# A Fourier neural operator on one core: the pointwise product of the inverse stage on four 64x64 tiles

## The chip, the cores and the metric

The kernel runs on one core of a Trainium2 chip. The metric is the device time of one launch in microseconds (us); lower is better. Engines are named as the profile names them: PE is TensorE (PEld its weight loads), DVE VectorE, ACT ScalarE, POOL GpSimd, SP SyncE, whose queue issues every transfer of the stages spoken of here.

## What is computed

Four layers of a Fourier neural operator on 32 images of 64x64 pixels and 64 channels, then a head, attention over 141 tokens and a mixture of experts. The change touches only the layers:

```python
h = jnp.einsum('bhwi,ic->bhwc', x, fc0_w) + fc0_b
h = h.transpose(0, 3, 1, 2)
for l in range(LAYERS):
    sc = _spectral_conv(h, w1r[l] + 1j * w1i[l], w2r[l] + 1j * w2i[l])
    pw = jnp.einsum('bihw,oi->bohw', h, pw_w[l]) + pw_b[l][None, :, None, None]
    y = sc + pw
    mean = y.mean(axis=(0, 2, 3), keepdims=True)
    var = y.var(axis=(0, 2, 3), keepdims=True)
    y = (y - mean) * jax.lax.rsqrt(var + EPS)
    y = y * gamma[l][None, :, None, None] + beta[l][None, :, None, None]
    h = jax.nn.gelu(y, approximate=False)
```

`_spectral_conv` is a real 2D FFT, a product of the 32x16 lowest modes with complex 64x64 matrices per mode, and the inverse FFT.

## The kernel before

Two images make a pair: partitions 0 to 63 hold the channels of the first, 64 to 127 those of the second, and 4096 columns hold the pixels. There are 16 pairs. Between stages the activations y lie in DRAM (`z_d`), the spectra in `X_d` and `G_d`. Each layer has three stages with a barrier between them: `fwd` (gelu of z, two forward transforms), `mix` (the product over the channels per mode) and `inv` (two inverse transforms, pointwise product, bias, statistics). Layer 0 has no `fwd` and no gelu: its z is the input x with 3 channels per image, and its pointwise weights are the product of the input layer and `pw_w`.

In `inv` a step is a quarter of a pair, 16 image rows or 1024 columns; a layer has 64 steps. Each engine runs a software pipeline written out by hand in `over_steps` and `step`: in turn n it works on step n minus a lag. All orders are fixed by this code, and semaphores carry the waits (`pI1`, `eI1`, `pT3`, `eT3`, `pY`, `eY`, `eS`, `z_gelu_c` count what PE, DVE and ACT have finished).

- PE, in each turn: four transposes of `Ai` (lag 5, line 371); in every second turn the first inverse transform (lag 1, L460), 16 matmuls of K = 64, 64 output rows and 128 columns on the four quarters of the array, `v` choosing the upper or lower half of the rows and `h`, the image, the half of the columns; then (lag 6) the pointwise product, two matmuls of K = 128 (block-diagonal weights `wbd` for two images; in layer 0 `wc6` with 96 rows) and 512 columns (L472); then the second inverse transform, eight matmuls that add to the same PSUM banks P[4] to P[7] (L477).
- DVE: copies the transposes to `ATs` (L738), the first transform from P[0] or P[1] to `Ai` (L743), and computes `bn_stats` of y (lag 7, L750).
- ACT: gelu of the loaded z in place (lag 4, L594, layers 1 to 3), then y = PSUM + bias into `ybuf` (lag 6, L604), two instructions of 512 columns per step.
- SP: in turn n, at the start of a pair four loads of `Gt` from `G_d` (L291), each 64 partitions; the store of step n - 8 from `ybuf` (L296), 128 partitions of 4 KB, after `eY`; the load of z for step n (L304; L302 for x in layer 0), after `pY` says that `zbuf` is free. `ybuf` has two buffers of one step.

Step q of a pair needs z columns q * 1024 to q * 1024 + 1023. The two PSUM banks of a step hold the upper and the lower two rows of each group of four, for both images.

## Time and profile before

| | |
|---|---|
| median of three runs | 3080.52 us (3080.41 to 3087.89) |
| the profiled execution | 3082.53 us, its span 3080.4 us |
| mean granted TensorE clock | 0.926 of full speed |
| PE busy | 2629.7 us (85%) |
| DVE busy | 1577.3 us (51%) |
| ACT busy | 1567.5 us (51%) |
| HBM read and written | 396 MB and 204 MB, 195 GB/s over the span |

The profile gives busy time per engine, the same in 40 slices of the span, the transfers, the chain of instructions that ended last, and groups of instructions by line. A PE group counts records: a matmul of float32 leaves two, a transpose one. The inverse stages lie at about 209 to 476, 789 to 1050, 1402 to 1650 and 1950 to 2215 us of the span.

### The profile page before, as it was taken

The numbers are of one execution on the slowest core, as the hardware profiler recorded it, in microseconds if no ns is written. First come the engines' busy times: TensorE is split into PE (matmuls) and PEld (weight loads), VectorE is DVE, ScalarE is ACT, GpSimd is POOL, SyncE is SP. The second block draws the span as 40 slices with busy tenths as digits, with TensorE's granted clock in tenths as the row PEclk, the third lists the DMA queues.
The fourth block names the chain that finished last, engine by engine and source line by source line (L and its number), as shares of the span: only waits on it lengthen the run. The fifth ranks groups of instructions, "written<-read, shape, count | busy, mean of one in ns | idle before, by whom it ended". The sixth has DMA issues, their size and how long they took to land. (4 is left out here: it accounts for less than half of the span.)

```text
span 3080.4 us, 65084 instructions
## 1 busy us (share of the span) xinstructions
PE 2629.7 (85%) x27131; PEld 1694.6 (55%) x27131; DVE 1577.3 (51%) x2552; ACT 1567.5 (51%) x2659; POOL 191.7 (6%) x237
## 2 busy tenths in 40 slices
PE   7559998978899899669998977899799577882999
PEld 4556665648566566566665657566422156642444
DVE  3136666752466677326666752466500376746443
ACT  1213336742456677225566753355499567851333
POOL 0000000000000000000000000000000222220443
PEclk9779999988899999889999998899899888995999
DMA  7845448966899799669988967799665200001432
GB/s 241 246 127 172 168 164 311 322 192 172 252 294 291 273 328 308 140 187 288 295 283 299 322 203 179 233 291 296 221 225 178 51 1 1 1 1 40 94 88 63
DMA packets 243649, 603.67 MB, mean 196 GB/s; under 512 B 28415, under 2 KB 108991, under 8 KB 241087
## 3 DMA queue, kind: packets, MB, share of 16 engines
q1 hardware_dynamic: 243359, 599.51, 62.7%
q8 instruction: 218, 3.57, 0.5%
q14 instruction: 72, 0.59, 0.1%
HBM read 396.12 MB, written 203.93 MB: 195 GB/s over the span
## 5 line engine op out<-in xcount | busy, mean ns | idle before, releaser
L604 ACT ACTIVATE work<-P,small 128x512 f32<-128x512 f32 x512 | 323.8, 683 | 536.0 <-PE P L477 499.3
L371 PE MATMUL P<-cst,work 128*128 128x128 f32 (+1 forms) x3760 | 547.3, 285 | 48.9 <-ACT work L626 13.7
L371 PEld LDWEIGHTS P<-cst,work 128*128 128x128 f32 (+1 forms) x3760 | 410.4, 143 | 206.6 <-issue 157.6
L426 PE MATMUL P<-W,work 128*64 128x64 f32 x4096 | 283.6, 307 | 129.9 <-ACT work L575 129.5
L472 PE MATMUL P<-work,wbd 128*128 128x512 f32 x768 | 371.5, 606 | 0.0
L477 PEld LDWEIGHTS P<-cst,ATs 64*128 64x128 f32 x4096 | 248.4, 187 | 194.1 <-issue 194.1
L426 PEld LDWEIGHTS P<-W,work 128*64 128x64 f32 x4096 | 282.0, 239 | 132.4 <-issue 98.7
L738 DVE COPY ATs<-P 128x512 f32<-128x512 f32 x256 | 177.0, 692 | 327.5 <-PE P L371 327.5
L750 DVE BATCH_NORM_STATS2 W<-work 128x6 f32<-128x512 f32 x512 | 327.1, 680 | 19.8 <-ACT work L604 19.2
L477 PE MATMUL P<-cst,ATs 64*128 64x128 f32 x4096 | 297.5, 285 | 0.0
L780 DVE COPY work<-P 128x512 f32<-128x512 f32 x384 | 247.1, 684 | 73.0 <-PE P L371 72.9
L594 ACT ACTIVATE work<-work,small 128x1024 f32<-128x1024 f32 x192 | 237.3, 1237 | 34.8 <-DMA work<-z_d 34.8
L626 ACT ACTIVATE work<-work,small 128x1024 f32<-128x1024 f32 x192 | 232.8, 1244 | 1.3 <-DMA work<-z_d 1.2
L743 DVE COPY work<-P 128x512 f32<-128x512 f32 x256 | 175.0, 686 | 110.6 <-PE P L460 110.6
L460 PE MATMUL P<-cst,work 64*64 64x128 f32 x4096 | 151.9, 289 | 55.6 <-DMA work<-G_d 49.6
L472 PEld LDWEIGHTS P<-work,wbd 128*128 128x128 f32 x768 | 131.4, 191 | 107.6 <-issue 107.3
L1463 DVE TENSOR_TENSOR mhid<-MH,ms 128x768 f32<-128x768 f32 (+1 forms) x96 | 90.4, 941 | 144.9 <-ACT ms L1389 116.9
L460 PEld LDWEIGHTS P<-cst,work 64*64 64x64 f32 x4096 | 119.1, 141 | 78.8 <-issue 61.1
L786 DVE COPY work<-P 128x512 f32<-128x512 f32 x192 | 132.7, 691 | 46.3 <-PE P L371 46.3
L719 DVE COPY work<-P 128x512 f32<-128x512 f32 x64 | 44.3, 693 | 212.3 <-PE P L426 130.9
L1134 ACT ACTIVATE aE<-AP,am 96x141 f32<-96x141 f32 x384 | 137.9, 380 | 29.0 <-DVE am L1184 28.4
L1389 ACT ACTIVATE ms<-MH 128x768 f32<-128x768 f32 (+1 forms) x96 | 76.5, 797 | 147.4 <-PE MH L1340 147.4
(166 smaller groups left out, 3031.2 us busy)
## 6 DMA issues: line engine op xcount, KB each, us to landing
work<-z_d SPq DMA_DIRECT2D x384, 512.0 KB, 6.0
z_d<-work SPq DMA_DIRECT2D x256, 512.0 KB, 4.0
W<-in_wmix SPq DMA_DIRECT2D x96, 512.0 KB, 6.8
X_d<-work SPq DMA_DIRECT2D x128, 256.0 KB, 5.0
work<-X_d SPq DMA_DIRECT2D x32, 1024.0 KB, 12.4
G_d<-work SPq DMA_DIRECT2D x128, 256.0 KB, 3.3
work<-G_d SPq DMA_DIRECT2D x256, 128.0 KB, 5.4
hz<-z_d SPq DMA_DIRECT2D x64, 512.0 KB, 4.6
```

The lines of the kernel that those rows point to most:

```text
L371: return nc.tensor.matmul(out, in_, ident[0:n, 0:n], start=True, stop=True, is_transpose=True)
L426: last = nc.tensor.matmul(P[n % 8][f * 64:f * 64 + 64, i * 64:i * 64 + 64], xm[:, :, x * 4 + y], W[:, 4 * (c + f) + y, x * 64:x * 64 + 64] ...
L460: last = nc.tensor.matmul(P[v][h * 64:h * 64 + 64, i * 128:i * 128 + 128], Gt[a.par][o, x:x + 64], i1c[o, v * 128:v * 128 + 128], start=Tr ...
L472: nc.tensor.matmul(banks[s][:, :].rearrange("p (j n) -> p j n", n=128), pw[0:rows, :], z[:, s], start=True, stop=False)
L477: last = nc.tensor.matmul(banks[s][:, j * 128:j * 128 + 128], ATs[o, a.q % 2, j * 128:j * 128 + 128], i2c[o, s * 128:s * 128 + 128], start ...
L594: nc.scalar.activation(z, z, ACT.Gelu, bias=bbi, scale=bsc).then_inc(S["z_gelu_c"], 1)
L604: nc.scalar.activation(y[:, h], P[4 + 2 * (a.q % 2) + h][:, :].rearrange("p (j n) -> p j n", n=128), ACT.Identity, bias=bias0 if first els ...
L626: nc.scalar.activation(zq[a.s % FR], zq[a.s % FR], ACT.Gelu, bias=bbi, scale=bsc).then_inc(S["z_gelu"], 1)
L738: nc.vector.tensor_copy(ATs[:, a.q % 2, :], P[2 + a.q % 2][:, :]).then_inc(S["eT3"], 1)
L743: nc.vector.tensor_copy(Ai[a.par].rearrange("p (y k) -> p y k", k=2 * KX)[:, :, v * KX + 8 * b:v * KX + 8 * b + 8], P[v][:, :].rearrange(" ...
L750: nc.vector.bn_stats(so, ybuf[a.q % 2][:, h * 512:h * 512 + 512]).then_inc(S["eS"], 1)
L780: nc.vector.tensor_copy(hTq[a.s % 2][:, h * 512:h * 512 + 512], P[h][:, :]).then_inc(S["eT1"], 1)
```

## The change

The pointwise product no longer takes two images as one block of 128 rows. Each image (`h`) and each half of the image's rows (`g`) gets its own 64x64 quarter of the array: four matmuls of K = 64 and 512 columns, with `h` choosing the rows of the array and `g` its columns. So the output partitions are now (half of the rows, channel), and a PSUM bank belongs to one image. Step q covers 8 rows of the upper half and the 8 rows 32 below.

What has to fit this layout:
- the constants `i1` are reordered and the first inverse transform (L460) runs as 32 matmuls of 64 columns instead of 16 of 128; its output partitions are (half, channel), and each group of 32 belongs to one image. DVE's copy to `Ai` takes runs of 16;
- `ybuf` has two buffers of 2048 columns, each for two steps of both images; SP stores them once in two steps, with two transfers, one from partitions 0 to 63 and one from 64 to 127 (`z_y`), so that `z_d` keeps its layout;
- z is loaded and passed to gelu in the order of columns 0, 2, 1, 3 (`QCOL`), and the product of step q waits for two gelus;
- in layer 0 x lies on partitions 0 to 2 and 64 to 66, with two loads per step, and the weights come from a product of 128x128 (`fcp`).

Core of the diff:

```diff
@@ -35,7 +35,9 @@
     f2[0, :, 0], f2[1, :, 0], f2[0, :, 1], f2[1, :, 1] = c, s, -s, c
-    i1 = np.kron(np.eye(2), np.block([[c.T, s.T], [-s.T, c.T]]))
+    i1 = np.block([[c.T, s.T], [-s.T, c.T]]).reshape(2 * KY, 2, 2, SIDE // 2).transpose(0, 2, 1, 3).reshape(2 * KY, 128)
+    i1 = np.kron(np.eye(2), i1)
     i2 = np.zeros((4, KX, 2, 4, SIDE))
@@ -112,14 +115,13 @@
         Gt = [part(14336, 1024), part(15360, 1024)]
-        ybuf = [part(16384, 1024), part(17408, 1024)]
+        ybuf = [part(12288, 2048), part(16384, 2048)]
         stats = W[:, WP - 1, 0:768]
...
         Xs0 = Xs + [part(0, 1024), part(1024, 1024)]
-        fc0Tbd = small[:, 16:22]
         fc0b_c, pwb_c, gam_c, bet_c = (small[:, i:i + 1] for i in range(4))
@@ -146,7 +148,10 @@
         z_q = z_d.rearrange("(t u) p (q n) -> t u p q n", u=2, q=4)
-        x6_q = x6.rearrange("(t u) p (q n) -> t u p q n", u=2, q=4)
+        x6_q = x6.rearrange("(t u) (h c) (q n) -> t u h c q n", u=2, h=2, q=4)
+        z_y = z_d.rearrange("(t u) (h o) (g k n) -> t u g k o h n", u=2, h=2, g=2, k=2)
+        QCOL = (0, 2, 1, 3)
@@ -196,6 +201,11 @@
+        def ychunk(a, h):
+            o = h * 1024 + a.q % 2 * 512
+            return ybuf[a.q // 2][:, o:o + 512]
         def over_steps(eng, body, last=PAIRS // 2 + 1):
@@ -290,21 +300,24 @@
                     b = At(t, u, q, 8)
-                    if b.ok:
+                    if b.ok and b.q % 2 == 1:
                         sp.wait_ge(S["eY"], l * 128 + b.s * 2 + 2)
-                        sp.dma_start(z_q[b.t, b.par, :, b.q], ybuf[b.q % 2]).then_inc(yst[b.q % 2], 16)
+                        for g in range(2):
+                            sp.dma_start(z_y[b.t, b.par, g, b.q // 2], ybuf[b.q // 2][g * 64:g * 64 + 64, :].rearrange("p (h n) -> p h n", h=2)).then_inc(yst[b.q // 2], 16)
                     if not a.ok:
                         return
-                    wait(sp, "pY", l * 128 + a.s * 2 - 14)
-                    o = slice(q * 1024, q * 1024 + 1024)
+                    if a.pair >= 2:
+                        sp.wait_ge(S["pY"], l * 128 + (a.pair - 2) * 8 + q // 2 * 4 + 4)
+                    o = slice(QCOL[q] * 1024, QCOL[q] * 1024 + 1024)
                     if first:
-                        sp.dma_start(zbuf[u][0:6, o], x6_q[a.t, u, :, q]).then_inc(zl[u][q], 16)
+                        for h in range(2):
+                            sp.dma_start(zbuf[u][h * 64:h * 64 + 3, o], x6_q[a.t, u, h, :, QCOL[q]]).then_inc(zl[u][q], 16)
                     else:
-                        sp.dma_start(zbuf[u][:, o], z_q[a.t, u, :, q]).then_inc(zl[u][q], 16)
+                        sp.dma_start(zbuf[u][:, o], z_q[a.t, u, :, QCOL[q]]).then_inc(zl[u][q], 16)
                 over_steps(sp, step)
                 for u in range(2):
-                    sp.wait_ge(yst[u], (l + 1) * 32 * 16)
+                    sp.wait_ge(yst[u], (l + 1) * 16 * 32)
                 leave(sp, "sp")
@@ -432,10 +445,10 @@
-                    nc.tensor.matmul(P[7][0:6, 0:128], fc0Tbd, wbd[:, :], start=True, stop=True)
+                    nc.tensor.matmul(P[7][:, 0:128], fcp[:, :], wbd[:, :], start=True, stop=True)
                     nc.tensor.matmul(P[6][:, 0:1], wbd[:, :], fc0b_c, start=True, stop=True).then_inc(S["pStat"], 1)
                     pe.wait_ge(S["eStat"], 1)
-                rows, pw = (96, wc6) if first else (128, wbd)
+                pw = wc6 if first else wbd
@@ -452,29 +465,30 @@
                         wait(pe, "eI1", l * 64 + a.s)
-                        for i in range(4):
-                            m = 2 * a.q + i
-                            for h in range(2):
+                        for m in range(8):
+                            for g in range(2):
                                 for v in range(2):
-                                    o, x = slice(v * 64, v * 64 + 64), h * 512 + m * 64
-                                    last = nc.tensor.matmul(P[v][h * 64:h * 64 + 64, i * 128:i * 128 + 128], Gt[a.par][o, x:x + 64], i1c[o, v * 128:v * 128 + 128], start=True, stop=True)
+                                    o, x, k = slice(v * 64, v * 64 + 64), a.q // 2 * 512 + m * 64, v * 128 + g * 64
+                                    last = nc.tensor.matmul(P[v][g * 64:g * 64 + 64, m * 64:m * 64 + 64], Gt[a.par][o, x:x + 64], i1c[o, k:k + 64], start=True, stop=True)
                         last.then_inc(S["pI1"], 1)
...
                         if first:
-                            pe.wait_ge(zl[a.par][a.q], a.t * 16 + 16)
+                            pe.wait_ge(zl[a.par][a.q // 2 * 2], a.t * 32 + 32)
+                            pe.wait_ge(zl[a.par][a.q // 2 * 2 + 1], a.t * 32 + 32)
                         else:
-                            pe.wait_ge(S["z_gelu_c"], (l - 1) * 64 + a.s + 1)
+                            pe.wait_ge(S["z_gelu_c"], (l - 1) * 64 + a.pair * 4 + a.q // 2 * 2 + 2)
                         wait(pe, "eY", l * 128 + a.s * 2 - 2)
                         banks = P[4 + 2 * (a.q % 2):6 + 2 * (a.q % 2)]
-                        z = zbuf[a.par][0:rows, a.q * 1024:a.q * 1024 + 1024].rearrange("p (j s n) -> p s j n", s=2, n=128)
-                        for s in range(2):
-                            nc.tensor.matmul(banks[s][:, :].rearrange("p (j n) -> p j n", n=128), pw[0:rows, :], z[:, s], start=True, stop=False)
+                        for g in range(2):
+                            for h in range(2):
+                                o, x = slice(h * 64, h * 64 + 64), g * 2048 + a.q * 512
+                                nc.tensor.matmul(banks[h][g * 64:g * 64 + 64, :], pw[o, o], zbuf[a.par][o, x:x + 512], start=True, stop=False)
                         pe.wait_ge(S["eT3"], l * 64 + a.s + 1)
                         for j in range(4):
-                            for s in range(2):
-                                o = slice(s * 64, s * 64 + 64)
-                                last = nc.tensor.matmul(banks[s][:, j * 128:j * 128 + 128], ATs[o, a.q % 2, j * 128:j * 128 + 128], i2c[o, s * 128:s * 128 + 128], start=False, stop=j == 3)
+                            for h in range(2):
+                                o = slice(h * 64, h * 64 + 64)
+                                last = nc.tensor.matmul(banks[h][:, j * 128:j * 128 + 128], ATs[o, a.q % 2, j * 128:j * 128 + 128], i2c[o, h * 128:h * 128 + 128], start=False, stop=j == 3)
                                 if j == 3:
@@ -588,20 +602,20 @@
                     c = At(t, u, q, 4)
-                    z = zbuf[c.par][:, c.q * 1024:c.q * 1024 + 1024]
+                    z = zbuf[c.par][:, QCOL[c.q] * 1024:QCOL[c.q] * 1024 + 1024]
                     if c.ok and not first:
-                        wait(act, zl[c.par][c.q], l * 128 + c.t * 16 + 16)
+                        wait(act, zl[c.par][c.q], 256 + (l - 1) * 128 + c.t * 16 + 16)
                         nc.scalar.activation(z, z, ACT.Gelu, bias=bbi, scale=bsc).then_inc(S["z_gelu_c"], 1)
...
                     if a.ok:
-                        y = ybuf[a.q % 2].rearrange("p (j s n) -> p s j n", s=2, n=128)
                         for h in range(2):
                             act.wait_ge(S["pY"], l * 128 + a.s * 2 + h + 1)
-                            if h == 0:
-                                wait(act, yst[a.q % 2], stores_waited(l, a))
-                                wait(act, "eS", l * 128 + a.s * 2 - 2)
-                            nc.scalar.activation(y[:, h], P[4 + 2 * (a.q % 2) + h][:, :].rearrange("p (j n) -> p j n", n=128), ACT.Identity, bias=bias0 if first else pwb_c).then_inc(S["eY"], 1)
+                            if h == 0 and a.pair >= 1:
+                                if a.q % 2 == 0:
+                                    act.wait_ge(yst[a.q // 2], (l * 16 + a.pair) * 32)
+                                act.wait_ge(S["eS"], l * 128 + a.s * 2 - 6)
+                            nc.scalar.activation(ychunk(a, h), P[4 + 2 * (a.q % 2) + h][:, :], ACT.Identity, bias=bias0 if first else pwb_c).then_inc(S["eY"], 1)
                 if first:
@@ -740,14 +750,14 @@
                         dve.wait_ge(S["pI1"], l * 32 + a.pair * 2 + b + 1)
-                        nc.vector.tensor_copy(Ai[a.par].rearrange("p (y k) -> p y k", k=2 * KX)[:, :, v * KX + 8 * b:v * KX + 8 * b + 8],
-                                              P[v][:, :].rearrange("p (k y) -> p y k", y=SIDE)).then_inc(S["eI1"], 1)
+                        nc.vector.tensor_copy(Ai[a.par].rearrange("p (y h z k) -> p h y z k", h=2, z=2, k=2 * KX)[:, b, :, :, v * KX:v * KX + KX],
+                                              P[v][:, :].rearrange("p (k y z) -> p y z k", k=KX, z=2)).then_inc(S["eI1"], 1)
                     a = At(t, u, q, 7)
...
                             so = stats.rearrange("p (t c) -> p t c", c=96)[:, a.t, a.par * 48 + (a.q * 2 + h) * 6:a.par * 48 + (a.q * 2 + h) * 6 + 6]
-                            nc.vector.bn_stats(so, ybuf[a.q % 2][:, h * 512:h * 512 + 512]).then_inc(S["eS"], 1)
+                            nc.vector.bn_stats(so, ychunk(a, h)).then_inc(S["eS"], 1)
                 over_steps(dve, step)
```

PE's instructions over two turns in the middle of layer 0, before (`wc` is the weight tile `wc6`, P the PSUM banks; x16 counts matmuls):

```order
L472 MATMUL P<-work,wc 128x512 x2
L477 MATMUL P<-cst,ATs 128x128 x8
L371 MATMUL P<-cst,work 128x128 x4
L460 MATMUL P<-cst,work 64x128 x16
L472 MATMUL P<-work,wc 128x512 x2
L477 MATMUL P<-cst,ATs 128x128 x8
L371 MATMUL P<-cst,work 128x128 x4
L472 MATMUL P<-work,wc 128x512 x2
```

and with the change, the same two turns, where the line numbers are those of the changed file:

```order
L486 MATMUL P<-work,wc 64x512 x4
L491 MATMUL P<-cst,ATs 128x128 x8
L384 MATMUL P<-cst,work 128x128 x4
L472 MATMUL P<-cst,work 64x64 x32
L486 MATMUL P<-work,wc 64x512 x4
L491 MATMUL P<-cst,ATs 128x128 x8
L384 MATMUL P<-cst,work 128x128 x4
L486 MATMUL P<-work,wc 64x512 x4
```

The order stays. Each product is four matmuls of 64 output rows instead of two of 128, each first transform 32 matmuls of 64 columns instead of 16 of 128.

SP's queue over one pair of images in layer 1, before (L291 loads the spectra, L296 stores y, L304 loads z):

```order
L291 DMA work<-G_d 64x512 [waits pI1]
L291 DMA work<-G_d 64x512 x3
L296 DMA z_d<-work 128x1024 [waits eY]
L304 DMA work<-z_d 128x1024 [waits pY]
L296 DMA z_d<-work 128x1024 [waits eY]
L304 DMA work<-z_d 128x1024 [waits pY]
L296 DMA z_d<-work 128x1024 [waits eY]
L304 DMA work<-z_d 128x1024 [waits pY]
L296 DMA z_d<-work 128x1024 [waits eY]
L304 DMA work<-z_d 128x1024 [waits pY]
```

and with the change:

```order
L301 DMA work<-G_d 64x512 [waits pI1]
L301 DMA work<-G_d 64x512 x3
L317 DMA work<-z_d 128x1024 [waits pY]
L307 DMA z_d<-work 64x2x1024 [waits eY]
L307 DMA z_d<-work 64x2x1024
L317 DMA work<-z_d 128x1024 [waits pY] x2
L307 DMA z_d<-work 64x2x1024 [waits eY]
L307 DMA z_d<-work 64x2x1024
L317 DMA work<-z_d 128x1024 [waits pY]
```

The eight transfers of z of a pair stay eight, and the loads of `G_d` stay four. The stores come two at a time after every second step, each from 64 partitions with two runs of 1024 columns, between two loads.

## Rows read from the trace of the kernel before

**Rows 1.** The page, parts 1 to 3: engines, 40 slices, the transfer queue.

```profile
PE 2629.7 (85%) x27131; PEld 1694.6 (55%) x27131; DVE 1577.3 (51%) x2552; ACT 1567.5 (51%) x2659; POOL 191.7 (6%) x237
...
PEclk9779999988899999889999998899899888995999
DMA  7845448966899799669988967799665200001432
...
q1 hardware_dynamic: 243359, 599.51, 62.7%
```

**Rows 2.** The view of stretches: 32 us of each inverse stage, layers 0 to 3.

```profile
core 0: us, PE busy (x) PEld busy (x) DVE busy (x) ACT busy (x) POOL busy (x), PEclk, DMA share, GB/s
262.00:294.00 32.00, 32.00 (x322) 19.76 (x322) 20.13 (x33) 10.12 (x16) 0.00 (x0) 1.00 0.49 170
862.00:894.00 32.00, 31.93 (x321) 19.88 (x320) 20.08 (x33) 19.13 (x24) 0.00 (x0) 1.00 0.93 295
1482.00:1514.00 32.00, 32.00 (x321) 19.79 (x320) 20.13 (x33) 19.03 (x25) 0.00 (x0) 1.00 0.93 296
2118.00:2150.00 32.00, 32.00 (x321) 19.81 (x320) 20.23 (x32) 19.13 (x24) 0.00 (x0) 1.00 0.94 301
```

**Rows 3.** The view of waits: who waited for whom, us in total, times, longest.

```profile
engine line waited for: us in total, times, longest us
...
ACT work L604 <- PE P L477: 499.3, 241, 32.7
```

**Rows 4.** Timeline of PE, two steps of layer 1; start us, duration us.

```profile
start us, us, engine line op out<-in xcount [idle before <-releaser]
907.00 0.66 PE L371 MATMUL P<-cst,work 128*128 128x128 f32 x4
907.58 1.10 PE L460 MATMUL P<-cst,work 64*64 64x128 f32 x32
908.62 1.98 PE L472 MATMUL P<-work,wbd 128*128 128x512 f32 x4
910.53 1.16 PE L477 MATMUL P<-cst,ATs 64*128 64x128 f32 x16
911.62 0.66 PE L371 MATMUL P<-cst,work 128*128 128x128 f32 x4
912.12 1.88 PE L472 MATMUL P<-work,wbd 128*128 128x512 f32 x4
913.93 1.16 PE L477 MATMUL P<-cst,ATs 64*128 64x128 f32 x16
915.02 0.66 PE L371 MATMUL P<-cst,work 128*128 128x128 f32 x4
915.61 0.34 PE L460 MATMUL P<-cst,work 64*64 64x128 f32 x4
```

**Rows 5.** Timeline of PE elsewhere: groups of matmuls on several tiles of the array.

```profile
621.35 0.66 PE L512 MATMUL P<-work,cst 64*32 64x256 f32 x16
...
1799.87 1.09 PE L534 MATMUL P<-work,cst 64*32 64x256 f32 x32
...
2302.04 1.06 PE L919 MATMUL HO<-hg,hfz 128*32 128x512 f32 x8
```

**Rows 6.** Groups by shape (busy us, mean ns); the last row is the timeline of L1329.

```profile
L426 PE MATMUL P<-W,work 128*64 128x64 f32 x4096 | 283.6, 307 | 129.9 <-ACT work L575 129.5 <-issue 0.4
...
L512 PE MATMUL P<-work,cst 64*32 64x256 f32 x3072 | 128.6, 392 | 1.9 <-DVE work L780 1.9
...
L1329 PE MATMUL MO<-mfold,macc 128*96 128x64 f32 x94 | 10.5, 254 | 0.5 <-ACT macc L1381 0.5
...
2899.29 0.89 PE L1329 MATMUL MO<-mfold,macc 128*96 128x64 f32 x8
```

**Rows 7.** The page, part 6: transfers by tile, KB of one, median us to landing.

```profile
work<-z_d SPq DMA_DIRECT2D x384, 512.0 KB, 6.0
z_d<-work SPq DMA_DIRECT2D x256, 512.0 KB, 4.0
```

**Rows 8.** Timeline: a load of x in layer 0; the start of layer 1.

```profile
245.29 0.32 SPq L302 DMA_DIRECT2D work<-in_x  x1
...
476.29 2.96 SPq L312 DMA_DIRECT2D work<-z_d  x6
...
482.81 2.37 ACT L626 ACTIVATE work<-work,small 128x1024 f32<-128x1024 f32 x2
```

**Rows 9.** Stretches: loads of 128 partitions, of 0 to 63; G_d, X_d stores; forward.

```profile
1646.00:1656.00 10.00, 9.47 (x107) 6.18 (x106) 6.67 (x11) 7.03 (x9) 0.00 (x0) 0.79 1.03 415
690.00:697.00 7.00, 0.16 (x2) 0.19 (x4) 2.12 (x2) 3.48 (x2) 0.00 (x0) 0.50 1.00 204
712.10:713.40 1.30, 1.30 (x24) 1.30 (x23) 0.69 (x1) 0.87 (x1) 0.00 (x0) 1.00 0.99 202
713.40:714.30 0.90, 0.90 (x18) 0.90 (x17) 0.00 (x0) 0.00 (x0) 0.00 (x0) 1.00 0.82 291
55.00:75.00 20.00, 19.01 (x42) 7.29 (x41) 7.77 (x20) 5.92 (x10) 0.00 (x0) 1.00 0.96 244
500.00:530.00 30.00, 30.00 (x492) 20.24 (x484) 22.90 (x42) 21.26 (x34) 0.00 (x0) 1.00 0.93 327
```

More of the change, by code:

```diff
@@ L84, in build_fno @@
         wbd = sb("wbd", [128, 128])
-        wc6 = sb("wc6", [96, 128])
+        wc6 = sb("wc6", [128, 128])
+        fcp = sb("fcp", [128, 128])
         P = [ctx.enter_context(nc.psum_tensor(f"P{i}", [128, 512], f32)) for i in range(8)]
@@ L236, in _ @@
                 o = slice(h * 64, h * 64 + 64)
-                sp.dma_start(fc0Tbd[o, h * 3:h * 3 + 3], fc0T).then_inc(S["s_w0"], 16)
+                sp.dma_start(fcp[o, h * 64:h * 64 + 3], fc0T).then_inc(S["s_w0"], 16)
                 sp.dma_start(fc0b_c[o, :], fc0b).then_inc(S["s_w0"], 16)
@@ L350, in _ @@
             nc.gpsimd.memset(small[:, :], 0.0)
-            nc.gpsimd.memset(wc6[:, :], 0.0)
+            nc.gpsimd.memset(fcp[:, :], 0.0)
             nc.gpsimd.memset(wbd[:, :], 0.0).then_inc(S["s_zero"], 1)
@@ L611, in inv @@
                 leave(act, "act")
-            def stores_waited(l, a):
-                return l * 32 * 16 + (a.pair * 2 + a.q // 2) * 16 if a.s >= 2 else 0
             def fwd(l):
@@ L725, in inv @@
                     dve.wait_ge(S["pStat"], 1)
-                    nc.vector.memset(work[0:96, 0:8192], 0.0).then_inc(S["z_zero"], 1)
+                    nc.vector.memset(work[:, 0:8192], 0.0).then_inc(S["z_zero"], 1)
                     dve.wait_ge(S["s_zero"], 2)
-                    link(nc.vector.tensor_copy(wc6[0:6, :], P[7][0:6, 0:128]))
+                    link(nc.vector.tensor_copy(wc6[:, :], P[7][:, 0:128]))
                 dve.wait_ge(S["s_parload"], (l + 1) * 128)
```

## Prediction

> **What bounds the kernel now.** I read the page first: PE is busy 85% of the span, DVE and ACT 51% each, and the DMA row stands at 8 or 9 tenths over long stretches [rows 1]. A share of the whole says little, so the next view is the table of stretches over the four inverse stages, the only ones that the change alters. In a steady 32 us of each, PE is busy for all of it at a granted clock of 1.00. In layer 0 the DMA engines stand at 0.49. In layers 1 to 3, which also read z back, they stand at 0.93 and 295 to 301 GB/s [rows 2]. PE is the bound there, and DMA is the next one, 7% behind. The waits agree: ACT's biggest wait is for the last inverse transform on PE [rows 3].
>
> The timeline gives the rhythm [rows 4]. Two steps, one with the first transform and one without, last from 907.58 to 915.61, so 8.03 us; 32 such pairs make a layer. Within a pair PE spends 1.04 us from start to start in the first transform (L460), then 1.91 and 1.81 us in the two pointwise products (L472), about 1.1 in each second transform (L477) and the rest in transposes (L371). DVE and ACT need about 20.1 and 19.0 us of 32, 5.0 and 4.8 per pair [rows 2].
>
> **The change on PE.** Pointwise product: two matmuls of 128x128 weights and 512 columns become four of 64x64 and 512 columns on the four quarters of the array. Each matmul leaves two records. The old form takes 1.88 to 1.98 us for its four records, because they follow one another [rows 4]. The nearest form with four tiles is L919 of the head, four column tiles of 512 columns: its eight records take 1.06 us. L460 shows that quarters of 64x64 overlap too (32 records in 1.10 us), and L534 that tiles may read different columns of the same partitions (32 records of 256 columns in 1.09 us) [rows 4, 5]. With the 0.07 us by which the next group starts before a row ends, a product costs 0.99 us and the pair saves 0.92 + 0.82 = 1.74 us. If the quarters did not overlap, eight records one after another would cost about 3.8 us per product; these three rows exclude it.
>
> First transform: 16 matmuls of 128 columns become 32 of 64 columns, 64 records for 32. The columns are the same in sum. Lower bound: nothing added. Upper bound: L426, also 64 columns wide, with 69 ns per record (283.6 us for 4096) on two tiles; with four that is 35 ns, 64 records take 2.2 us, and 1.2 us is added. Between them lies L1329: one tile, 64 columns but 96 columns of weights, (0.89 - 0.25) / 7 = 0.09 us each [rows 6]. Scaled to 64 columns of weights and spread over four tiles this is 0.015 us, or 0.97 us for 64 records, no more than the 1.04 of now. I take zero. The Trainium skill (TensorE: Matmul & The Clock Gate, Back-to-back issue gap) puts a floor of about 25 ns under small matmuls; 64 of them would be 1.6 us, and the sum for layer 0 would be 18 us less favourable. L512 does not bear it out: its 16 records last 0.66 us together and 0.39 us each, so they start within 0.27 us, 18 ns apart [rows 5, 6].
>
> Modes: the gap between L460 and L472 goes, and one between transposes and product comes in each step, where now the product starts 0.16 us before the transposes' row ends, against 0.08 for L460 [rows 4]. I put +0.08 us per pair. PE needs 8.03 - 1.74 + 0.08 = 6.37 us per pair.
>
> **What hides the rest.** The DVE copy of the first transform writes runs of 16 instead of 8 from a PSUM read that stays strided; the ACT eviction has the same 512 elements per partition. Both cost nothing, under PE's 6.37 us against 5.0 and 4.8. The product of step s now needs the gelu of s + 1, which ACT runs one turn earlier. The set-up (one wider memset, one 128-column product) happens once. The queue on SP keeps its twelve issues per pair of images in layers 1 to 3, but the store waits for two steps, and the load ahead of it for one step more of PE. Loads are issued six turns before their gelu; a store has one turn more than before until its buffer is needed, about 3 x 3.2 - 1.3 = 8 us even at PE's new pace, against a landing of 4.0 us for one of 512 KB [rows 7]. In layer 0 the small loads double, from one issue to two, each 0.32 us of SP. At the end of a layer the last store is twice as large and the next stage's loads wait for it. They are issued at 476.29 and ACT's first gelu starts at 482.81, behind the statistics, so with a landing of 6.0 us the cover is about 0.5 us [rows 7, 8]; without it a layer loses 1 to 2 us. I leave this out of the sum.
>
> **The change on the DMA engines.** Bytes stay the same: 295 GB/s x 8.03 us = 2.37 MB per pair of steps. Their present need is 0.93 x 8.03 = 7.47 us in layers 1 to 3 and 0.49 x 8.03 = 3.93 us in layer 0. But each store now covers 64 partitions instead of 128, 1.05 MB per pair. Loads over all partitions run at 415 GB/s with the engines full; loads into partitions 0 to 63 run at 204 GB/s, also full. G_d's stores, which come in halves, run at 202 GB/s for partitions 0 to 63 and at 291 for 64 to 127, and X_d's, which alternate the halves in 512-byte packets, at 244 [rows 9]. So the price x of the halves, per pair: below, nothing (the 291 GB/s is no half, and X_d beats 204); above, 1.05 / 0.204 - 1.05 / 0.415 = 2.6 us. G_d's two stores of 0.26 MB took 1.30 + 0.90 us; four of these are 4.4 us against 2.5, so x = 1.9 for stores that stand alone. In a queue that is never empty, one half's packets run beside the other's and beside full-width loads; I take a third of it, x = 0.6. This is the least certain number here. The need becomes 7.47 + 0.6 = 8.07 us in layers 1 to 3, above PE's 6.37: **DMA becomes the bound, at the old pace**. In layer 0 it is 4.5, still under PE.
>
> The Trainium skill speaks against the change here (SBUF — State Buffer, Door 1): partitions 0 to 63 reach only 8 of the 16 ports, and two transfers on the two halves do not add up. By that rule every half store runs at half rate, which is the 2.6 us above. The load row of 204 GB/s agrees with it; the store row of 291 does not.
>
> **The sum.** Layer 0: 32 x (6.37 - 8.03) = -53 us. Layers 1 to 3: 96 x (8.07 - 8.03) = +4. Together -49. The profiled execution took 3082.5 us (span 3080.4), 2.0 above the median of 3080.5: 3033.5 against itself, 3031 against the median.
>
> **The rivals.**
> Half stores cost their isolated price (slower). With x = 1.9 the DMA need is 9.37 us, layers 1 to 3 lose 96 x 1.34 = 129 us, layer 0 still gains 53, and the time is 3157. With x = 2.6 it is 10.07 us, +196, and layer 0 gains 48: 3229. It decides where 96 (x - 0.56) passes 53, at x = 1.11. For it: G_d's first halves and the loads into one half [rows 9]. Against it: G_d's second half, and X_d. Chance 0.33.
> The halves cost nothing and the queue packs better. The forward stage holds 327 GB/s over 30 us [rows 9]; at that rate a pair takes 2.37 / 0.327 = 7.25 us, layers 1 to 3 gain 75, the sum is -128: 2952. Were DMA no bound at all, 128 x 1.66 = 212 would come off: 2868. Chance 0.20.
> The first transform pays its upper bound: PE 7.57 us, layer 0 gains 15 and the others stay: about 3069. Chance 0.05. If the tiles did not overlap, each pair would grow by some 4 us and the kernel by 500; under 0.01.
> Gain and loss cancel (x near 1.1), between 3071 and 3090: 0.08.
> The forecast, 3005 to 3070: 0.34.
>
> **The numbers.** A measurement of this kernel can tell 0.3%, 9 us, from no change. Faster: 0.34 + 0.20 + 0.05 = 0.59. Same: 0.08. Slower: 0.33. The range must reach into both big rivals: 2940 takes in the better queue, 3165 the isolated price; outside are the unbound case and the full half rate, 2 in 10. The forecast's own range is 3005 to 3070.
>
> **What would show it.** Right: a pair of 6.3 to 6.5 us in layer 0 with PE still busy throughout; product rows of eight records near 1.0 us; in layers 1 to 3 a pair near 8.1 us, DMA share at 1.0, PE with gaps, and ACT's eviction waiting for the z_d store. Wrong: layers 1 to 3 well under 7.6 us per pair (the halves are free), or over 8.4 with the DMA rate under 280 GB/s (they are not); a first transform over 1.5 us; or a layer 0 that waits for anything but PE.

## The result, and the profile after

The kernel with the change takes **3182.4 us** (median of 4 runs, 3177.7 to 3184.6) against 3082.0 for the kernel before on the same chip: ratio 1.032, 95% interval 1.030 to 1.034. It is slower by 100 us, where 3031 was forecast, and outside the forecast's outer range of 2940 to 3165.

The profiled execution has a span of 3175.6 us. The page, parts 1 and 6, beside [rows 1] and [rows 7]:

```profile
PE 2511.6 (79%) x32251; PEld 1645.9 (52%) x32251; DVE 1576.0 (50%) x2552; ACT 1567.9 (49%) x2659; POOL 191.7 (6%) x237
...
z_d<-work SPq DMA_DIRECT2D x256, 512.0 KB, 6.1
```

PE does its work in 118 us less than before, so the arithmetic was saved, and the time still grew. The store of 512 KB lands in 6.1 us instead of 4.0 [rows 7].

The view of stretches, from the first to the last y eviction of each inverse stage, layers 0 to 3. Counted in evictions such a stretch has 31.6 pairs of steps, and that is the divisor of the figures per pair below, unless a middle is named. The loads and first transforms of the first steps stand ahead of the stretch, so these figures come out some per cent under the steady rhythm (250.04 / 31.6 = 7.91 for the 8.03 of [rows 4]):

```profile
core 0: us, PE busy (x) PEld busy (x) DVE busy (x) ACT busy (x) POOL busy (x), PEclk, DMA share, GB/s
221.15:445.79 224.64, 202.01 (x3616) 129.64 (x3615) 155.84 (x246) 80.24 (x128) 0.00 (x0) 0.98 0.74 182
781.46:1066.65 285.19, 223.08 (x3616) 143.33 (x3616) 155.88 (x246) 148.92 (x188) 0.00 (x0) 0.87 0.84 241
1401.62:1687.69 286.07, 226.50 (x3616) 146.15 (x3616) 155.82 (x246) 149.03 (x188) 0.00 (x0) 0.87 0.83 241
2022.87:2308.30 285.43, 224.79 (x3616) 144.78 (x3616) 155.88 (x246) 149.04 (x189) 0.00 (x0) 0.87 0.83 241
```

and the same stretches of the kernel before, of which layers 0 and 1 stand for all:

```profile
223.01:472.82 249.81, 249.19 (x2436) 153.64 (x2435) 155.84 (x246) 80.28 (x127) 0.00 (x0) 1.00 0.48 166
802.63:1052.67 250.04, 249.36 (x2436) 153.83 (x2436) 156.26 (x246) 148.98 (x188) 0.00 (x0) 1.00 0.87 279
```

Layer 0 gained 25 us, each of layers 1 to 3 lost 34 to 36, together +80. PE was busy through a stage before; now it stands still for a tenth of layer 0 and over a fifth of the others. The DMA engines are not full either, at 0.84 and 241 GB/s. The other 15 us of the 95 by which the spans differ lie between the stretches: from the end of one to the start of the next it takes 335.7 us (445.79 to 781.46) where it took 329.8, and 4 to 5 us more at the two other places. At the first place the next layer's loads are issued 7.8 us after the last two evictions began, where it was 4.1, and the first gelu starts 13.2 us after them instead of 10.6 (timelines of both): 2.6 of the 5.9 us. The rest was not traced.

The view of waits, beside [rows 3]:

```profile
ACT work L618 <- PE P L491: 614.5, 253, 32.6
...
PE P L472 <- DMA work<-G_d: 252.6, 59, 13.6
...
PEld P L472 <- DMA work<-G_d: 224.1, 55, 6.0
```

PE and its weight loads (PEld) wait in the same pauses, so the two rows count the same time twice: PE stands for 253 us waiting for the **G_d loads**, not for their sum of 477, which the expectations below use. About 42 us of it is the start of the four inverse stages, where the kernels with the loads in time wait as well (42.2 us in four waits in e15); the kernel before has 49.6 us in nine. So some 210 us are lateness, in which no term of the prediction had a part.

Where PE does not wait, the timeline of layer 0 shows the pair as forecast, beside [rows 4]:

```profile
323.42 1.09 PE L486 MATMUL P<-work,wc 64*64 64x512 f32 x8
...
326.12 1.16 PE L472 MATMUL P<-cst,work 64*64 64x64 f32 x64
327.10 1.04 PE L486 MATMUL P<-work,wc 64*64 64x512 f32 x8
...
329.75 1.09 PE L486 MATMUL P<-work,wc 64*64 64x512 f32 x8
```

From 323.42 to 329.75 it is 6.33 us.

**Where the loads are late.** One pair of images in layer 1: SP's queue, and then PE.

```profile
890.51 0.33 SPq L317 DMA_DIRECT2D work<-z_d  x1
891.76 1.24 SPq L307 DMA_DIRECT2D z_d<-work  x2
893.04 1.86 SPq L317 DMA_DIRECT2D work<-z_d  x1
894.94 4.51 SPq L301 DMA_DIRECT2D work<-G_d  x4
899.50 0.58 SPq L317 DMA_DIRECT2D work<-z_d  x1
```

```profile
886.02 1.99 PE L472 MATMUL P<-cst,work 64*64 64x64 f32 x64 [4.70 <-DMA work<-G_d]
...
903.79 1.99 PE L472 MATMUL P<-cst,work 64*64 64x64 f32 x64 [3.74 <-DMA work<-G_d]
905.56 1.93 PE L486 MATMUL P<-work,wbd 64*64 64x512 f32 x8
```

Read as one chain from wait to wait, this is a closed loop. PE gets its G_d at 886.02; the transform, the product and the second transform behind it, and ACT's eviction (890.47 to 891.73 on ACT's timeline) let SP issue two stores at 891.76 (5.74 us after 886.02); the stores and one load of z are issued until 894.94 (3.18 us); the four G_d loads take 4.51 us to issue; the last lands and PE goes on at 903.79 (4.34 us). That is 17.77 us for a pair of images, two pairs of steps, or 8.9 each. It is the shortest round of this layer: the twelve from 806.10 to 1039.76 take 233.66 us, 19.5 each or 9.7 per pair of steps, and in each of them PE waits 3.5 to 5.8 us for G_d. The first rounds of the layer, up to 794.60, still run at 6.33 us without a wait, which is why the stretch as a whole gives 9.03. PE's own work ends in a group of transposes at 899.40, so it would have been ready at about 900: from the store at 891.76 the chain has 8.2 us and needs 12.0. In these 12.0 us the DMA engines stand at 0.91, in the 5.7 before them at 0.80 (view of stretches): the loop puts PE's work and the transfers' one behind the other. In the kernel before the same three links read

```profile
896.96 0.32 SPq L296 DMA_DIRECT2D z_d<-work  x1
897.33 1.35 SPq L304 DMA_DIRECT2D work<-z_d  x1
898.72 2.62 SPq L291 DMA_DIRECT2D work<-G_d  x4
```

with L460 at 907.58 [rows 4]: 10.6 us from the store. The issues take 4.4 of them, and the last load, issued at 900.7, lands 5.4 us later (view of L291), 9.1 us after the store. There was a slack of 1.5 us. The change cut the time on offer by 2.4 us, as PE is faster, and lengthened the chain by 2.9; the sum, 3.8 us too late, is the wait of 3.74. Each pause also costs clock. After it the granted clock falls (0.75 over the 5.74 us from 886.02), and the next transform and product last 1.99 and 1.93 us in place of 1.16 and 1.04; in layers 1 to 3 the granted clock is 0.87, and PE is busy for 223 to 226 us with the instructions that take 202 in layer 0, at 0.98.

### The profile page after: what moved, and what is told of

It reads as the page before. It is cut to its first block and busy times, and to the rows that moved or that the text cites. A ratio compares the mean times of both kernels' runs of the same rounds, so it can differ in the third digit from the quotient of the medians.

```text
span 3175.6 us, 75376 instructions
## 1 busy us (share of the span) xinstructions
PE 2511.6 (79%) x32251; PEld 1645.9 (52%) x32251; DVE 1576.0 (50%) x2552; ACT 1567.9 (49%) x2659; POOL 191.7 (6%) x237
## 5 line engine op out<-in xcount | busy, mean ns | idle before, releaser
L472 PE MATMUL P<-cst,work 64*64 64x64 f32 x8192 | 192.9, 260 | 261.0 <-DMA work<-G_d 252.6
L491 PEld LDWEIGHTS P<-cst,ATs 64*128 64x128 f32 x4096 | 267.7, 200 | 241.0 <-issue 132.9
L472 PEld LDWEIGHTS P<-cst,work 64*64 64x64 f32 x8192 | 172.5, 170 | 287.0 <-DMA work<-G_d 224.1
L491 PE MATMUL P<-cst,ATs 64*128 64x128 f32 x4096 | 318.0, 298 | 0.0
L486 PE MATMUL P<-work,wbd 64*64 64x512 f32 x1536 | 239.0, 697 | 0.0
L940 PE MATMUL HP<-hz,hf 64*128 64x512 f32 x512 | 134.9, 639 | 15.3 <-ACT hz L908 14.9
```

What stands on the lines that cost most here:

```text
L472: last = nc.tensor.matmul(P[v][g * 64:g * 64 + 64, m * 64:m * 64 + 64], Gt[a.par][o, x:x + 64], i1c[o, k:k + 64], start=True, stop=True)
L486: nc.tensor.matmul(banks[h][g * 64:g * 64 + 64, :], pw[o, o], zbuf[a.par][o, x:x + 512], start=True, stop=False)
L491: last = nc.tensor.matmul(banks[h][:, j * 128:j * 128 + 128], ATs[o, a.q % 2, j * 128:j * 128 + 128], i2c[o, h * 128:h * 128 + 128], start ...
```

## Experiments

The letters are those of the expectations, and e2 stands for the run whose name begins so. In short, **A** blames the width of the stores (64 partitions each), **B** the order, in which the G_d loads stand in SP's queue right behind two stores. The kernel before was run beside each batch (3084 to 3087 us); ratios are to it.

### Earlier G_d loads, in the change and in the kernel before

```diff
-                    if q == 0 and a.ok:
-                        wait(sp, "pI1", l * 32 + a.pair * 2 - 2)
+                    e = At(t, u, q, -2)
+                    if e.q == 0 and e.ok:
+                        wait(sp, "pI1", l * 32 + e.pair * 2 - 2)
...
-                                sp.dma_start(Gt[u][v * 64:v * 64 + 64, h * 512:h * 512 + 512], G_s[h, a.t, u, v]).then_inc(gl[u], 16)
+                                sp.dma_start(Gt[e.par][v * 64:v * 64 + 64, h * 512:h * 512 + 512], G_s[h, e.t, e.par, v]).then_inc(gl[e.par], 16)
```

The loads of the first pair are issued ahead of the loop.

> The changed kernel, with one edit: the four G_d loads of a pair are issued two turns earlier on SP (the first pair's before the loop). Stores stay split by half. Both theories say that PE's wait for G_d shrinks from 477 us to under 100. Theory A says that the slow half stores then show as transfer need: about 7.6 us per two steps in layers 1 to 3, so a pair takes 7.6 to 8.2 us there and 6.4 in layer 0; total 3000 to 3045. Theory B says that the halves cost nothing once the order is mended: layers 1 to 3 at 7.0 to 7.3; total 2930 to 2960.

> The kernel before with its G_d loads issued two turns earlier, as in e2_gload_two_turns_early. Theory A (the loads became late by the change; in the kernel before PE waits for them for 59.8 us in the whole program, and its layers 1 to 3 run at a DMA need of 6.9 us per pair under a PE need of 8.0): 3055 to 3085 us. Rival (loading G_d earlier is worth its 170 us in this kernel whatever the tiles): 2900 to 3000 us.

Measured: the change with early loads takes **3008.6 us**, ratio 0.976 (0.974 to 0.977), the kernel before with them 3073.3, 0.997 (0.996 to 0.998). So lateness of these loads cost 174 us (PE's wait for them falls from 252.6 to 42.3 us), and only in the kernel with the change; the 10 us in the other come from between the stages, its layers 1 to 3 keep their 250 us. The stretches of layers 0 and 1 of the first:

```profile
219.50:435.02 215.52, 201.76 (x3616) 130.65 (x3615) 153.69 (x246) 78.77 (x127) 0.00 (x0) 0.98 0.76 189
767.58:1003.20 235.62, 205.03 (x3616) 132.07 (x3616) 155.75 (x246) 147.55 (x188) 0.00 (x0) 0.97 0.98 295
```

Now the DMA engines are full in layer 1, at 235.62 / 31.6 = 7.46 us per pair. ACT's eviction now waits 261.5 us for PE and also

```profile
ACT work L623 <- issue: 182.7, 54, 7.1
```

With no engine behind it, this is read as the eviction waiting for the store that still holds its buffer; the view does not name the store. That is the state that the prediction had described for the change itself. Theory A had put layers 1 to 3 at 7.6 to 8.2 us per pair (7.8 in the middle of layer 1, see below) and layer 0 at 6.4. Layer 0 stands at 6.8: there SP waits for only 17 us of the 190 from 230 to 420 us, its issues follow one another, and PE waits 12.8 us for evictions.

### Stores of full width

The two stores of 64 partitions cannot simply be cut by image instead. That was tried first:

```diff
-                        for g in range(2):
-                            sp.dma_start(z_y[b.t, b.par, g, b.q // 2], ybuf[b.q // 2][g * 64:g * 64 + 64, :].rearrange("p (h n) -> p h n", h=2)).then_inc(yst[b.q // 2], 16)
+                        for h in range(2):
+                            sp.dma_start(z_h[b.t, b.par, h, b.q // 2], ybuf[b.q // 2][:, h * 1024:h * 1024 + 1024]).then_inc(yst[b.q // 2], 16)
```

> The changed kernel, with one edit: the two stores after each second step are split by image instead of by half of the rows, so that each covers all 128 partitions (half a store is 1024 columns of each). Bytes, packets, places in SP's queue and all waits stay. Theory A (stores of 64 partitions take twice as long per packet, hold up the one queue, and the G_d loads behind them reach PE too late): the packets of the stores go back to about 159 ns, PE's wait for G_d in the first transform falls from 477 us to under 150, layer 0 runs at 6.4 us per two steps, layers 1 to 3 at 7.3 to 7.8; total 2940 to 3000 us. Theory B (the order is at fault: two stores and two loads in one burst, one turn later than before): the waits for G_d stay above 350 us and the total stays above 3130.

> Both edits: stores by image, G_d loads two turns earlier. Both theories: no wait for G_d; layer 0 at 6.35 us per two steps, layers 1 to 3 between PE's 6.35 and the transfer need of 6.9 to 7.2; total 2900 to 2960. Theory A: at least 40 us under the kernel with early loads alone. Theory B: the same as that within 10 us.

Measured: 4941 and 4931 us, ratios 1.60 both, with early loads and without. A stretch of layer 0 of the first, and its wait:

```profile
300.00:500.00 200.00, 79.19 (x1172) 50.11 (x1172) 46.17 (x73) 22.32 (x36) 0.00 (x0) 0.66 0.17 66
...
ACT work L618 <- issue: 1901.8, 120, 18.1
```

The DMA share is 0.17 at 66 GB/s while ACT waits for the stores. The rows of an image's half lie in two blocks of z_d, so this store's pattern has 2 as its outermost dimension. The Trainium skill (DMA: Bandwidth & Descriptors, Why a DMA increments its semaphore by 16 and not by 1) says that a transfer is spread over the largest number of engines up to 16 that divides the outermost dimension of both of its sides. The two sides have 2 and 128 here, which by that page is two engines, an estimate of 0.125 of the 16. The 0.17, with the other transfers beside the stores, is near it; no view of these runs tells one DMA engine from another. As a test of A these runs say nothing.

So the stores were given full width at the price of their place: same bytes, same wait, 128 rows outermost. The two kernels with this edit (e7, e8) write z_d in an order that the next layer does not read, so they do not compute what the reference does; they do the same instructions on the same number of bytes, and only their times are used.

```diff
-                        for g in range(2):
-                            sp.dma_start(z_y[b.t, b.par, g, b.q // 2], ybuf[b.q // 2][g * 64:g * 64 + 64, :].rearrange("p (h n) -> p h n", h=2)).then_inc(yst[b.q // 2], 16)
+                        for h in range(2):
+                            sp.dma_start(z_q[b.t, b.par, :, b.q // 2 * 2 + h], ybuf[b.q // 2][:, h * 1024:h * 1024 + 1024]).then_inc(yst[b.q // 2], 16)
```

> The change, with its two stores of 64 partitions replaced by two stores of 128 partitions and the same bytes, at the same place, after the same wait. To keep 128 rows outermost they go to other places of z_d than the reference's layout asks for; the work and the bytes are those of the change. Theory A (the width of the stores, 0.6 to 1.5 us of DMA time per pair of steps, keeps the queue full, and the G_d loads come late for that): packets at 160 ns again, 2960 to 3080 us. Rival B (the order: two stores in one burst every second turn ahead of the G_d loads, whatever their width): 3130 to 3190 us. Theory C, between: 3080 to 3130.

> As e7_full_width_stores (z_d written in another layout), with the G_d loads two turns earlier as well. Theory A (with the loads in time the width of the stores is what is left of the DMA's need, 7.5 us per pair of steps against 6.9 before): 2900 to 2965 us, layers 1 to 3 at 6.9 to 7.1 us per pair. Rival (the width costs nothing once the loads are in time): 2995 to 3020 us, as e2_gload_two_turns_early.

Measured: 3069.2 us, 0.995 (0.993 to 0.997), and with early loads **2903.1 us**, 0.941 (0.940 to 0.943). Stretches of layers 0 and 1, first of e7, then of e8:

```profile
220.51:418.00 197.49, 196.48 (x3616) 127.11 (x3615) 155.87 (x246) 80.22 (x127) 0.00 (x0) 1.00 0.58 209
752.24:1013.57 261.33, 219.72 (x3616) 139.86 (x3616) 155.87 (x246) 148.98 (x189) 0.00 (x0) 0.90 0.81 265
```

```profile
220.67:417.61 196.94, 196.33 (x3616) 127.11 (x3615) 155.88 (x246) 80.22 (x127) 0.00 (x0) 1.00 0.58 209
748.25:957.40 209.15, 199.10 (x3616) 128.42 (x3616) 156.46 (x246) 147.48 (x189) 0.00 (x0) 1.00 0.97 334
```

The two edits give four kernels: 3182.4 with neither cure, 3008.6 with early loads (-174), 3069.2 with full width (-113), 2903.1 with both (-279). The two costs nearly add up. The three that are new lie in A's ranges for the total, e7 near the upper end of its own and e8 near the lower, and B alone is excluded by e7. But A's reason, that the loads are late because of the width, holds for layer 0 only, where full width alone removes the whole loss. In layers 1 to 3 of e7 the loop stays closed (8.3 us per pair), and PE still waits (the whole program, in which about 42 us are the starts of the stages):

```profile
PE P L472 <- DMA work<-G_d: 177.4, 47, 13.7
```

So width and order each cost by themselves.

### Half stores in the kernel before

```diff
-                        sp.dma_start(z_q[b.t, b.par, :, b.q], ybuf[b.q % 2]).then_inc(yst[b.q % 2], 16)
+                        for g in range(2):
+                            sp.dma_start(z_q[b.t, b.par, g * 64:g * 64 + 64, b.q], ybuf[b.q % 2][g * 64:g * 64 + 64, :]).then_inc(yst[b.q % 2], 16)
```

> The kernel before, with one edit: each store of a step is issued as two of 64 partitions. Theory A: packets of partitions 0 to 63 near 310 ns, the transfer need rises by about 0.6 us per two steps to 7.5 of 8.03, and PE, which has less slack to fill here, waits a little for G_d: total 3085 to 3140. Theory B: no change, 3075 to 3090.

Measured: 3093.5 us, 1.003 (1.002 to 1.004). Layers 0 and 1:

```profile
223.33:473.14 249.81, 249.19 (x2436) 153.64 (x2435) 155.82 (x246) 80.41 (x128) 0.00 (x0) 1.00 0.63 166
805.48:1059.89 254.41, 249.62 (x2436) 153.81 (x2436) 157.34 (x246) 149.10 (x188) 0.00 (x0) 1.00 0.89 273
```

In layer 0 the same bytes keep the engines busy for 0.63 of the time instead of 0.48, 157 us instead of 120, or +1.2 us per pair; in layer 1 for 0.89 of 254.41 instead of 0.87 of 250.04, +0.3 us. All of it but 8 us is hidden behind the slower PE. These stores are of 256 KB; the change's are of 512 KB.

### How much lead, or what stands ahead

> The change with its G_d loads one turn earlier (two turns gave 3008.6 us against 3182.4 without). Theory A (what counts is by how much the loads lead the product; one turn is half a pair's half, about 1.6 us, and the wait removed by it is most of 477 us when the load stood right behind the stores): 3040 to 3120 us. Rival (the loads are early enough as soon as they stand ahead of the stores of the same turn): 3000 to 3020 us.

> The change with its G_d loads four turns earlier. Theory A (with two turns nothing waits for G_d any more and the DMA engines are busy 97% of layers 1 to 3, so more lead gives nothing): 2995 to 3020 us. Rival (there are still late loads in the 7.5 us that a pair of steps takes there): 2940 to 2990 us.

Measured: one turn 2998.4 us, 0.972 (0.970 to 0.973); four turns 2972.8, 0.963 (0.962 to 0.965). One turn gave all that two gave, against theory A of that expectation: it already takes the loads past the two stores. To tell lead from order, the loads were left in their turn and the stores moved one turn later, behind them:

```diff
-                    b = At(t, u, q, 8)
+                    b = At(t, u, q, 9)
```

> The change with its z_d stores issued one turn later, so that in a turn with both the G_d loads stand ahead of the stores instead of right behind those of the turn before; the G_d loads keep their turn. Theory O (order: the loads are late because two stores and their condition stand right ahead of them): 2990 to 3060 us. Theory L (lead: the load's turn is too near to the product's): 3140 to 3190 us. The stores have a turn less until ACT needs their buffer, which may add 0 to 60 us to either.

Measured: **3001.5 us**, 0.972 (0.971 to 0.974). SP's queue in layer 1 of this kernel, and its stretch:

```profile
887.55 1.38 SPq L317 DMA_DIRECT2D work<-z_d  x2
888.98 3.14 SPq L301 DMA_DIRECT2D work<-G_d  x4
892.16 1.27 SPq L307 DMA_DIRECT2D z_d<-work  x2
```

```profile
774.26:1004.53 230.27, 207.42 (x3616) 133.08 (x3616) 156.47 (x246) 146.64 (x188) 0.00 (x0) 0.96 0.95 299
```

It is the order, in the sense of the loop: no store with its wait for an eviction stands right ahead of the G_d loads any more, and they are issued in 3.14 us. A number 8 that becomes 9 (and one more round of the loop, for the last store) brings back 181 us, nearly all of it in layers 1 to 3; layer 0 gains 5 us (219.70) and then waits for evictions (16.2 us), for G_d only 1.3. The four turns bring another 26, against the expectation: in e14 PE still waits 57 us for G_d, in 21 waits, in e15 42 us in 4. That is not the whole reason, since with two turns it is 42 us in 5 and the time 36 us longer than with four; PE's wait for gelus falls as well (66.1, 54.7 and 42.1 us with two, one and four turns), and why was not tested.

With four turns the loads stand in SP's queue where the change has them, behind two stores and a load of z, but a pair of images ahead:

```profile
864.89 1.78 SPq L312 DMA_DIRECT2D z_d<-work  x2
866.72 1.37 SPq L322 DMA_DIRECT2D work<-z_d  x1
868.13 5.40 SPq L306 DMA_DIRECT2D work<-G_d  x4
```

So the place behind the stores is dear only with the short lead. Order and lead are two ways to open the same loop.

### The stores on another queue

> The change, with its z_d stores issued by POOL instead of SP, at the same condition; the loads stay on SP with their order and their place. Theory A1 (the G_d loads are late because they stand behind the stores in SP's queue): 3000 to 3090 us. Rival A2 (they are late because the DMA engines are busy with the stores' packets, whoever issued them, and one turn is too short): 3140 to 3200 us. If POOL's own queue is dearer to issue from, both times rise by what its issues show.

> e11_stores_by_pool (3027.9 us) with the G_d loads two turns earlier too. Theory A (both cure the same lateness; DMA work of 6.7 us per pair of steps, as e11 shows, is then the bound of layers 1 to 3): 2900 to 2960 us. Rival (POOL's stores arrive late by themselves, ACT waits for them): 2990 to 3030 us.

> e2_gload_two_turns_early (3008.6 us) with the store of partitions 64 to 127 issued by ACT after its eviction, that of 0 to 63 by SP as before, so that the two halves can be in flight together. Theory H (two halves that move together take no longer than one store of the whole width): 2905 to 2960 us. Rival A (a half store's packets cost the engines the same whichever runs beside it): 3000 to 3025 us. If ACT's issues are held up by a full queue as SP's are (up to 2.3 us each), more: 3030 to 3100 us.

> e12_stores_by_pool_gload_early (2953.7 us) with the G_d loads four turns earlier instead of two. If the DMA engines are what bounds layers 1 to 3 (they were busy for 96 to 97% there, 6.8 us of work per pair of steps): 2935 to 2955 us. If late G_d loads still cost something there: 2900 to 2935 us.

The edit of e11 moves the wait and both stores, unchanged, from SP's program to POOL's, in a loop of its own, and e12 and e20 are that with the G_d loads two and four turns early. That of e17 takes e2 and moves the store of partitions 64 to 127 to ACT, behind the eviction. Measured: e11 3027.9 us, 0.982 (0.980 to 0.984); e12 2953.7, 0.957 (0.955 to 0.959); e17 2964.0, 0.961 (0.959 to 0.962); e20 **2933.6**, 0.950 (0.948 to 0.952).

With the G_d loads left in place, taking the stores off SP's queue brings 155 us (e11): A1, they stood behind the stores. It is not all of the lateness, since PE still waits 146.5 us for G_d there. Layers 0 and 1 of e17, then of e20:

```profile
219.81:416.88 197.07, 196.45 (x3616) 127.22 (x3615) 156.22 (x246) 80.35 (x128) 0.00 (x0) 1.00 0.83 207
748.73:975.19 226.46, 206.11 (x3616) 132.42 (x3616) 156.48 (x246) 149.96 (x188) 0.00 (x0) 0.98 0.99 308
```

```profile
222.09:419.05 196.96, 196.35 (x3616) 127.13 (x3615) 155.59 (x246) 80.25 (x127) 37.41 (x62) 1.00 0.80 207
751.77:966.93 215.16, 200.10 (x3616) 129.18 (x3616) 155.76 (x246) 146.83 (x188) 37.19 (x62) 0.99 0.96 326
```

Two halves on two queues are not cheaper for the engines, so theory H's reason fails, although e17 missed its range for it by only 4 us, and that of rival A by 36: 0.83 x 197.07 / 31.6 = 5.2 us of DMA per pair in layer 0, where two halves on one queue take 0.76 x 215.52 / 31.6 = 5.2 and full width 0.58 x 196.94 / 31.6 = 3.6. But layer 0 now runs at PE's pace with half-width stores. So there the halves cost through SP's queue, not through the engines. e20 came out at the border of its two ranges: four turns still bring 20 us, with the engines at 0.96, and each pair needs 0.96 x 215.16 / 31.6 = 6.5 us of them where e12 needed 6.8. Why the same packets took less time there was not looked into. Of the kernels that compute what the reference does e20 is the fastest, 4.8 to 5.2% under the kernel before.

## Why the prediction was wrong, by its own steps

- **The change on PE: right.** Pair 6.37 forecast, 6.33 measured. Product 0.99 forecast; from start to start 1.02 and 0.97. First transform +0 us: 0.98 from start to start against 1.04, so the zero held; the upper bound of +1.2 us and the floor cited beside it did not come. Layer 0 at -53 us is what e7, e8, e17 and e20 give (197 us against 249.8).
- **What hides the rest: wrong, and this is the step that failed.** It listed the queue's issues and worked out the slack of z's loads ("six turns before their gelu") and of the stores (8 us), and not that of the third user of the queue. The G_d loads had 1.5 us to spare, in the round that was read. I had gone through the queue by what had changed in it; the load that stood unchanged was the one whose predecessor had changed. e19 shows the cost by moving nothing but the stores: 181 us, where the sum had 0.
- **The change on the DMA engines: the price was near, the need of full engines was not.** x = 0.6 was forecast; in the change it is 0.84 x 285.19 / 31.6 = 7.6 us against 0.87 x 250.04 / 31.6 = 6.9, +0.7, and e2 against e8 (7.3 and 6.4) +0.9. In layer 0 it is 5.3 against 3.8, +1.5, toward the isolated price of 1.9. The need of 7.47 was read rightly, but at a share of 0.93, and the sum took it that engines at 1.00 would need as long. The middle of layer 1, twenty pairs of steps each, in the kernel before, e2 and e8:

```profile
850.80:1011.40 160.60, 160.53 (x1601) 99.35 (x1602) 101.49 (x160) 95.63 (x120) 0.00 (x0) 1.00 0.93 296
814.20:970.00 155.80, 132.77 (x2401) 86.33 (x2402) 101.24 (x160) 94.71 (x121) 0.00 (x0) 0.97 1.00 303
788.90:925.30 136.40, 128.84 (x2402) 83.51 (x2400) 101.58 (x160) 94.58 (x120) 0.00 (x0) 1.00 1.02 349
```

  That is 8.03, 7.79 and 6.82 us per pair: with the engines full, the bytes take 6.8 us at full width (349 GB/s) and 7.8 with half stores (303 GB/s), where 7.47 and 8.07 stood in the sum. This is the "better queue" of the second rival, and the halves took all of it back. Had the loads been in time, the change would have been worth about 75 us (e2), 79 in the stretches. The forecast of 49 is near that by luck: layer 0 gives 34 of its 53, and layers 1 to 3 gain 45 (part of it at the ends of the stage, where the rhythm is not that of the middle) where +4 was forecast. "DMA becomes the bound" is true of e2, not of the change, where it stands at 0.84.
- **The end of a layer**: "1 to 2 us", left out; the first gelu of layer 1 came 2.6 us later. Between the stretches 4 to 6 us per layer were added, 15 in all, the rest of them untraced.
- **The rivals.** The time is near that of the first (3157), yet it is not that rival: it needed a full DMA queue and x = 1.9. None of them had a late transfer as its mechanism.
- **The signs.** "Over 8.4 us with the DMA rate under 280 GB/s" did come, and was put down beforehand to half stores at full price; only 105 to 113 of the 279 us between the change and e8 are theirs. The sign that spoke truly was the last: a layer 0 that waits for anything but PE.

## What to carry to other kernels

In an in-order queue, compute the slack of every transfer, not of those the change edits: from the last wait that stands ahead of it to its use, and look whether that wait depends on the work that the transfer feeds. If it does, the chain is a loop whose length is the rhythm, and a faster engine only runs into it. Issue loads ahead of a conditional store of the same turn, and take a DMA share of 0.84 beside an idle PE as a reason to look for such a loop before calling it a bound.

## What the runs showed of the hardware that was not expected

- The time of an issue on SP depends on what stands ahead of it: behind two half stores one load of z took 1.86 us and four G_d loads 4.51, against 1.35 and 2.62 in the same places of the queue before. The Trainium skill (DMA: Bandwidth & Descriptors, Issuing engines are not separate DMA queues) says that issuing from several engines saves only the time on the sequencer, usually small beside the transfer. The engines' work agrees (5.2 us per pair of layer 0 either way), but the time saved was 45 us (e2 to e17), 18 of them in layer 0, where SP in e2 hardly ever waits. That SP's issues were what held the rest up is the reading of this; the other 27 us were not looked into.
- Stores of 64 partitions (1.05 MB per pair) add to the DMA engines' work whichever queue they come from, and most in layer 0, where the engines are otherwise slack: 1.2 to 1.6 us per pair there, 0.3 to 0.9 in layers 1 to 3. The same bytes took 6.8 us per pair with full engines and 7.5 at a share of 0.93 (e8 and the kernel before).
- 64 records of 64 columns on the four quarters of the array take 0.98 us from start to start, 15 ns each.
